# A reordered key scratch read in two loads of 48 rows, and the loads of all x blocks moved behind the tables

## The reference, cut to what matters

```python
q = (x @ wq).reshape(B, S, 16, 16)      # 16 query heads of 16
k = (x @ wk).reshape(B, S, 4, 16)       # 4 key/value heads
v = (x @ wv).reshape(B, S, 4, 16)
q, k = rope(q), rope(k)
scores = einsum('bqkgd,bskd->bkgqs', q.reshape(B, S, 4, 4, 16), k) / 4
out = einsum('bkgqs,bskd->bqkgd', softmax(scores), v).reshape(B, S, 256) @ wo
x = layernorm(x + out)
x = layernorm(x + ffn(x))               # silu gate, 256 -> 1024 -> 256, dequantized integer weights
```

## Time and profile before

| | us |
|---|---|
| median of 3 runs | 902.65 |
| lowest and highest | 902.3, 905.37 |
| profiled execution: its own time | 899.15 |
| profiled execution: span, first to last instruction | 897.3 |
| TensorE busy | 881.7 (98%) |
| VectorE busy | 741.9 (83%) |
| ScalarE busy | 712.9 (79%) |
| GpSimd busy | 268.6 (30%) |
| DMA queue of SP | 50280 packets, 65.53 MB, 28.4% of 16 engines |

### The profile page before, as it was taken

How to read it: one execution, slowest core, us unless ns; L and a number is a source line. 1 busy time by engine, 2 the same in 40 slices (tenths; PEclk the granted TensorE clock), 3 DMA queues, 4 the chain that set the end, 5 groups by cost and what they waited for, 6 DMA issues and landing times.

```text
span 897.3 us, 16216 instructions
## 1 busy us (share of the span) xinstructions
PE 881.7 (98%) x5658; PEld 460.2 (51%) x5658; DVE 741.9 (83%) x1655; ACT 712.9 (79%) x929; POOL 268.6 (30%) x232
## 2 busy tenths in 40 slices
PE   9999999999999999999999999999999999999996
PEld 3334444444444444444444444444436888888885
DVE  5577999999999999999999999999955455665545
ACT  2467999999999999999999999999985566555564
POOL 7763430035434000001001000210104665665555
PEclk9997999999999999999999999999999999999998
DMA  8973553323443132232223313121112010110001
GB/s 265 295 205 113 130 123 79 90 81 77 99 124 61 45 77 64 56 73 67 52 54 85 73 46 78 45 67 32 37 55 57 25 48 24 48 47 25 24 24 48
DMA packets 53458, 69.98 MB, mean 78 GB/s; under 512 B 17344, under 2 KB 26560, under 8 KB 53376
## 3 DMA queue, kind: packets, MB, share of 16 engines
q1 hardware_dynamic: 50280, 65.53, 28.4%
q0 software_dynamic: 864, 3.15, 1.2%
q10 hardware_dynamic: 2232, 0.25, 0.2%
HBM read 46.74 MB, written 16.25 MB: 70 GB/s over the span
## 4 chain that ended last, share of the span: by engine, by line
PE 89%; DVE 4%; ACT 2%; issue 2%; DMA 1%; SPq 1%; POOL 0%; POOLq 0%; DVEq 0%; ACTq 0%
PE pv_bank L1374 26%; PE ring_bank L1286 24%; PE pair_bank L1432 13%; PE pair_bank L1500 12%; PE pv_bank L1526 3%; PE ring_bank L1526 3%; PE ring_bank L1384 2%; PE pair_bank L1320 2%; DVE block_max L851 2%; ACT probs L1187 1%; DMA q_parts<-low 1%; PE ring_bank L1399 1%; PE pv_bank L1338 1%; DVE above L847 0%; PE pv_bank L1264 0%
## 5 line engine op out<-in xcount | busy, mean ns | idle before, releaser
L1187 ACT ACTIVATE probs<-pair_bank 128x1024 f32<-128x1024 f32 x512 | 495.7, 1023 | 43.2 <-PE pair_bank L1432 43.1
L851 DVE TENSOR_REDUCE block_max<-ring_bank 128x1 f32<-128x384 f32 x854 | 486.7, 609 | 15.4 <-PE ring_bank L1286 6.0
L1286 PE MATMUL ring_bank<-k_max,q_sb 48*128 48x512 f32 x1127 | 313.3, 445 | 1.8 <-DVE block_max L847 0.7
L1286 PEld LDWEIGHTS ring_bank<-k_max,q_sb 48*128 48x128 f32 x1127 | 150.2, 185 | 267.5 <-DVE block_max L851 116.8
L1374 PE MATMUL pv_bank<-probs,v_all 128*17 128x512 f32 x2048 | 270.5, 600 | 0.6 <-ACT probs L1187 0.5
L1432 PE MATMUL pair_bank<-q_sb,k_sb 50*128 50x512 f32 x1024 | 221.5, 428 | 1.2 <-ACT probs L1187 0.7
L1042 DVE SCALAR_TENSOR_TENSOR hid<-pair_bank,up_s,silu 128x512 f32<-128x512 f32 x63 | 47.1, 748 | 85.0 <-ACT silu L1243 85.0
L1432 PEld LDWEIGHTS pair_bank<-q_sb,k_sb 50*128 50x128 f32 x1024 | 99.1, 186 | 29.5 <-ACT probs L1187 7.4
L760 POOL TENSOR_TENSOR hid_l<-hid,hid_h 128x512 fp32r<-128x512 f32 x63 | 81.7, 1297 | 86.3 <-ACT hid_h L1222 85.6
L675 POOL TENSOR_TENSOR attn<-attn,inv_rows 128x1024 f32<-128x1024 f32 x7 | 16.7, 2388 | 300.8 <-DMA inv_rows<-inv_d 228.5
L847 DVE CUSTOM_DVE_ANT_0 above<-ring_bank,above 128x512 f32<-128x512 f32 x137 | 94.0, 688 | 5.7 <-PE pair_bank L1286 3.6
(11 more groups left out here) (142 smaller groups left out, 862.0 us busy)
## 6 DMA issues: line engine op xcount, KB each, us to landing
k_max<-k_parts SPq DMA_DIRECT2D x96, 96.0 KB, 3.6
q_sb<-q_parts SPq DMA_DIRECT2D x64, 128.0 KB, 3.4
k_sb<-k_parts SPq DMA_DIRECT2D x96, 64.0 KB, 2.3
attn<-xT SPq DMA_DIRECT2D x8, 512.0 KB, 5.4
q_parts<-high SPq DMA_DIRECT2D x16, 256.0 KB, 3.7
q_parts<-low SPq DMA_DIRECT2D x16, 256.0 KB, 4.1
q_sb<-q_parts SPq DMA_DIRECT2D x64, 64.0 KB, 3.5
attn<-pv_sb SPq DMA_DIRECT2D x128, 32.0 KB
```

The source lines that it names most:

```text
L851: dve.reduce_max(block_max[half % 2][:, col:col + 1], bank[:, 0:width], axis=AX.X).then_inc(ring_used, 1)
L1187: act.activation(probs[t % 2][:, 2 * pr:2 * pr + 2, :], pair_bank[pr][:], ACT.Exp, scale=D ** -0.5).then_inc(probs_ready, 1)
L1286: pe.matmul(bank[:, 0:last - first], q_sb[k][rows, i, qt * P:(qt + 1) * P], k_max[k // QH][rows, kind * CH + first:kind * CH + last], star ...
```

## The change

The scratch of keys gets an axis for the combination, and its order is now sequence, chunk, combination, row, position. The high part is stored twice, as combinations 0 and 1. `load_k` then reads 48 rows in one DMA, once for each row group. A DMA of a key store now covers 64 rows and one chunk, so that `store_k` issues six DMAs instead of two and `store_gap` three instead of two. x blocks 2 to 7 are all issued behind the tables and the identity, and the loads between the stores are gone.

```diff
-K_LOADS = 16 * GROUPS * COMBOS
+K_LOADS = 16 * GROUPS
+K_STORES = 16 * COMBOS * 2
+GAP_STORES = 16 * COMBOS
...
-        k_parts = nc.dram_tensor("k_parts", (B, 2, QH + 1, D * HKV, CH), fp32).ap()
+        k_parts = nc.dram_tensor("k_parts", (B, QH + 1, COMBOS, D * HKV, CH), fp32).ap()
...
             head = UNITS * pair + s
+            src = k_parts[head // HKV, 0:parts].rearrange("c m (d h) t -> c (m d h) t", h=HKV).rearrange("c (n h) t -> h n c t", h=HKV)[head % HKV]
             for r in range(GROUPS):
-                for combo, part in enumerate((0, 0, 1)):
-                    src = k_parts[head // HKV, part, 0:parts].rearrange("c (d h) t -> d h c t", h=HKV)[:, head % HKV]
-                    row = r * GROUP + combo * D
-                    queue.dma_start(dst[s][row:row + D].bitcast(fp32).rearrange("d (c t) -> d c t", c=parts), src).then_inc(done[s], 16)
+                rows = dst[s][r * GROUP:r * GROUP + ROWS].bitcast(fp32).rearrange("n (c t) -> n c t", c=parts)
+                queue.dma_start(rows, src).then_inc(done[s], 16)
...
             load_x(1)
             load_q_tables(1)
-            load_x(2)
             sp.dma_start(ident[:], identity).then_inc(ident_loaded, 16)
+            for m in range(2, BLOCKS):
+                load_x(m)
...
-                for part, buf, ready in ((0, high_k, k_hi_ready), (1, low_k, k_lo_ready)):
+                for buf, ready, combos in ((high_k, k_hi_ready, (0, 1)), (low_k, k_lo_ready, (2,))):
                     sp.wait_ge(ready, b + 1)
-                    sp.dma_start(k_parts[b, part, 0:QH].rearrange("c r t -> (c r) t"), buf[:].bitcast(fp32)).then_inc(k_stored[b], 16)
+                    for combo in combos:
+                        for c in range(QH):
+                            src = buf[c * HKV * D:(c + 1) * HKV * D].bitcast(fp32)
+                            sp.dma_start(k_parts[b, c, combo], src).then_inc(k_stored[b], 16)
...
                 for part, buf, ready in ((0, gap_h, gap_h_ready), (1, gap_l, gap_l_ready)):
                     sp.wait_ge(ready, b + 1)
-                    sp.dma_start(k_parts[b, part, QH], buf[:].bitcast(fp32)).then_inc(gap_stored, 16)
+                    for combo in ((0, 1), (2,))[part]:
+                        sp.dma_start(k_parts[b, QH, combo], buf[:].bitcast(fp32)).then_inc(gap_stored, 16)
...
                         store_gap(0)
-                    if m + 3 < BLOCKS:
-                        load_x(m + 3)
                     if m == 2:
                         first_loads()
```

More of the change, by code:

```diff
@@ L398, in first_loads @@
                 load_q(0, 0, sp)
-                sp.wait_ge(k_stored[0], 16 * 2)
-                sp.wait_ge(gap_stored, 16 * 2)
+                sp.wait_ge(k_stored[0], K_STORES)
+                sp.wait_ge(gap_stored, GAP_STORES)
                 sp.wait_ge(memsets, 6)
@@ L542, in attention @@
                         if k == 0 and p % 2:
-                            sp.wait_ge(k_stored[(p + 1) // 2], 16 * 2)
-                            sp.wait_ge(gap_stored, 16 * 2 * ((p + 1) // 2 + 1))
+                            sp.wait_ge(k_stored[(p + 1) // 2], K_STORES)
+                            sp.wait_ge(gap_stored, GAP_STORES * ((p + 1) // 2 + 1))
                         load_k(k_max, p + 1, k // QH, kmax_loaded, sp)
@@ L628, in high_of_k @@
                 pool.wait_ge(k_rot_ready, b + 1)
-                pool.wait_ge(k_stored[b - 1], 16 * 2)
+                pool.wait_ge(k_stored[b - 1], K_STORES)
                 pool.tensor_copy(high_k[:], rotated_k[:]).then_inc(k_hi_ready, 1)
@@ L638, in gap_of @@
                 pool.tensor_tensor(k_half[:], rotated_k[0:HKV * D, :], k_half[:], ALU.subtract).then_inc(k_gap_ready, 1)
-                pool.wait_ge(gap_stored, 16 * 2 * b)
+                pool.wait_ge(gap_stored, GAP_STORES * b)
                 pool.wait_ge(k_gap_ready, b)
@@ L666, in _ @@
             for b in range(B):
-                pool.wait_ge(k_stored[b], 16 * 2)
-            pool.wait_ge(gap_stored, 16 * 2 * B)
+                pool.wait_ge(k_stored[b], K_STORES)
+            pool.wait_ge(gap_stored, GAP_STORES * B)
             pool.wait_ge(v_used, 2 * B)
```

## The result

| | before | after |
|---|---|---|
| median of 4 runs, us | 902.47 | 929.08 |
| lowest and highest | 902.1, 905.37 | 926.72, 931.12 |
| profiled execution, its own time | 899.15 | 931.12 |

The changed kernel is slower: its time is 1.0287 of that of before, 95% interval 1.0254 to 1.0319, 26.6 us. The forecast was 901.5, with 904.8 as the upper end.

A forecast was written before the change was run, and what follows sets the result against it. TensorE, busy 98% of the span, was taken to bound the kernel, with only the projections open to gain. The 0.80 and 0.35 us gaps sum to 1.15: 902.65 - 1.15 = 901.5 us, range 898.0 to 904.8.

The forecast's parts named there:

- Nothing waits there in a way that a transfer could mend: Attention: TensorE's waits from 80 us on are 1.8 us in total, none on a DMA, so sooner or fewer transfers change nothing.
- The 115.7 us of SP: Attention: given as SP's longest wait, for VectorE's shift, to show that SP stands ahead of its work.
- the cost of nothing for the loads in attention: Attention or beside it: 186 load DMAs become 62, 56 us less of SP's time, costed at nothing.
- TensorE shows waits on a DMA in attention: Sign of being wrong, in attention: it would break the cost of nothing given to SP's part.
- The gain of 1.15 us in the projections: End of projections: TensorE's 0.80 us wait for the first k_max and a 0.35 us gap both go.
- the second gap: TensorE's 0.35 us before 39.68 us, released by ScalarE, late behind a store; it was to go too.
- my bounds (30.5 to 32.5): Start in us of the first k_max loads on SP; the value taken was 31.05.
- The other landing that the prediction names: First k_max: by ports, 48 rows move at most 217 GB/s, landing near 37.4, 0.8 us of the sum unpaid.
- Rival A: Start of attention: the half-clock stretch, some 3 us, goes (898.5 us) or a second comes (904.5); chance 0.2.
- the x blocks in front are paid for: Queue before the first k_max: 1.43 MB added, yet k_max lands at 36.3 us, before TensorE asks at 36.53.
- rival B's late stores: SP's queue, 12 to 38 us: block 0's stores land after 23.6, k_max at 39 to 40; +1.7 to +2.7 us; chance 0.15.
- fifteen more stores in pair 0 fit in: Pair 0 of attention: five more in each of three halves, 3 us each, only shorten SP's waits; cost nothing.

The follow-up runs named there:

- x_back: The changed kernel with the x blocks loaded where they were before; scratch, stores and the two loads of 48 rows stay; 929.5 us, ratio 1.0312.
- x_only: The kernel before with only the loads of the x blocks moved behind the tables; 901.54 us, ratio 0.9982.
- x_late: The kernel before with x blocks moved to the front and k_max in attention loaded only when the next half's shift has landed; 899.44 us, ratio 0.9939.
- x_ahead: The kernel before with x blocks in front and the last shift write moved from ScalarE's queue to SP's, ahead of k_max; 899.61 us, ratio 0.9955.
- late_kmax: The changed kernel with one more SP wait: k_max in attention is loaded only when the next half's shift has landed; 901.66 us, ratio 0.9987.
- shift_ahead: The changed kernel with the last shift write of a half moved from ScalarE's queue to SP's, ahead of k_max; 899.37 us, ratio 0.9956.
- long_rows: The changed kernel with a scratch where a row's chunks are neighbours, so 288 KB come in 48 pieces instead of 144; 922.92 us, ratio 1.0221.
- two_and_one: The changed kernel with each k_max load cut in two DMAs, 192 KB and 96 KB; 910.06 us, ratio 1.0062.
- six_loads: The changed kernel with each key operand loaded from the new scratch by six DMAs of 16 rows instead of two of 48; 907.87 us, ratio 1.0056.

## Why the prediction was wrong, point by point

**"Nothing waits there in a way that a transfer could mend": true of the list of waits, not of the kernel.** The list shows neither what is nearly late nor what is late by a tenth or two. In attention it has no wait on a transfer, and I took that for room. The last shift write had 2.92 us from issue to use at the boundary above, and its landing was what ended them. The 115.7 us of SP that the prediction calls its longest wait are 31 waits, the longest 7.1 us: SP does stand ahead of its work, but that says nothing of a write from ScalarE's queue.

**The step that failed is the cost of nothing for the loads in attention.** "Elsewhere 186 DMAs of such loads become 62 [...] I cost that at nothing." I counted SP's time, which is what merging saves, and looked for who waits behind SP. I did not count what a merged DMA does to the other queue. The text even named the cover whose loss would break it ("TensorE shows waits on a DMA in attention"), and gave it no price and no chance. It should have been a rival: place, each half with `k % QH == 0`; price, the time that 192 KB more take on the DMA engines; point from which it decides, the margin of the last shift write. In hindsight, from part 6 of the two pages: the `k_max` DMAs land after 5.1 us in the median, and after 3.6 before, so some 1.5 us in each of up to 14 halves, some 20 us. Measured were 15.7 us in 12, and 13 us of lower clock behind them. The rows for it were in the trace: both queues' issues around one boundary, and the distance to the matmul that uses them.

**The gain of 1.15 us in the projections didn't come either.** SP did finish its `k_max` issues earlier, at 32.84 instead of 33.73, and the store of q's low part was issued at 33.48 instead of 34.36. The first maximum still came at 37.52 with 0.60 us of wait, for 37.34 with 0.80 in the earlier trace rows (TensorE ended its projections at 36.92 here, for 36.53), and the second gap stayed at 0.33. Of the term of 1.15 us, 0.2 is what the waits became shorter:

```profile
37.52 0.46 PE L1290 MATMUL pair_bank<-k_max,q_sb 48*128 48x512 f32 x1 [0.60 <-DMA k_max<-k_parts]
...
39.84 0.50 PE L1290 MATMUL pair_bank<-k_max,q_sb 48*128 48x512 f32 x1 [0.33 <-ACT above L1134]
```

ScalarE's high part began at 38.67, behind a store that took 5.1 us to land instead of 4.1. What I won in issues was lost in landings. That the large load in front delays the store behind it, as it does the shift later, is the likely reason; no run isolates it here. I had let the landing time stand at what it was while the load grew to three times its size. The two loads were begun at 32.06, inside my bounds (30.5 to 32.5) but a microsecond past the value that I took, because SP's key and gap stores took their issue time there. x_back shows the other half of the account: with the new stores and loads and the x blocks at their old places `k_max` is 2.14 us late and ScalarE waits 4.8 us for its store, while x_only has 0.33 and 2.5. So moving x helped, the stores and the loads took it back. The kernels agree among themselves: x_late and x_ahead, with x_only's projections, wait 0.38 and 0.37 us, and late_kmax and shift_ahead, with the changed kernel's, 0.58 and 0.95. The other landing that the prediction names, near 37.4 with 0.8 us unpaid, fits the start at 37.52, but says nothing of the rows of a load: x_only's six loads of 16 rows give a start at 37.49.

**The clock.** Rival A looked at the half-clock stretch at the start of attention and whether it would go. It is what the waits bring about that mattered: of the 12 waits five were followed by a stretch at the lower clock, 29 us in all, and these cost nearly as much as the waits, 13 us. The stretch at the start neither went nor came from the change. By the Trainium skill (TensorE: Matmul & The Clock Gate, section "HAM oscillation — how this bites in real kernels") idle stretches of TensorE behind a DMA are what sends its clock down, and the penalty is half of the slow time. The trace agrees with the penalty, about 0.45 us for one. For the first it shows that each of the five falls stands behind a wait on a DMA of 1.4 to 1.8 us, and that seven other such waits, of 0.5 to 1.6 us, were followed by none. In long_rows two of 12 were, and of the six in two_and_one none.

**Right** were only that the x blocks in front are paid for (rival B's late stores didn't come: no L1097 waited for a store near 23 to 27 us), and that fifteen more stores in pair 0 fit in, as long as the loads are two; six_loads shows that beside six loads they don't.

## What to carry to other kernels

Merging DMAs saves time on the queue that issues them, and can take it from a small transfer that another queue issues just behind. Before a load is made larger, look for the latest small write on the other queues, measure from its issue to its first use, and put the large load behind it in program order, or cut it. And where the list of waits is empty, read one boundary instruction by instruction: no margin at all looks the same in it as one of ten microseconds.

## What was not expected of the hardware

A small DMA from one queue stands behind a large one that another queue issued just before, and the longer the larger that is. Packets that started in the trace of the changed kernel, by quarter microsecond: `k_max` from SP's queue (2 KB packets) and ScalarE's third and fourth shift writes (16 packets of 128 bytes each, issued at 206.50 and 207.26):

```
from us   k_max   shift from ScalarE's queue
 208.00      0    16
 208.25      0     0
 208.50      3     0
 208.75      5     0
 209.00     25     0
 209.25     35     0
 209.50     38     5
 209.75     23    11
```

The third write moved 1.6 us after its issue. So late after its own the fourth would have moved near 208.9, when 8 packets of `k_max` had been started. It moved after 2.5 us, when 103 had been, most of the 144 of the first DMA. At the other eleven boundaries with a wait 89 to 235 had been, so in six of the twelve some of the second DMA's too, which was issued after the write. In the kernel before the fourth moved 1.7 to 1.8 us after its issue, behind 37 of a DMA's 48 packets. By the Trainium skill (DMA: Bandwidth & Descriptors, section "Issuing engines are not separate DMA queues") DMAs of different engines run on the same 16 DMA engines and interleave: that they share them is what this case shows. By the same page of the Trainium skill (section "Queues, rings and completion order") each DMA engine changes between queues only at the end of a packet, and a packet is typically some 9 to 17 descriptors. A descriptor there is one run of bytes, what this trace lists as a packet. As an estimate from that page: the 144 runs of a `k_max` DMA are 9 for each of 16 engines, so an engine may move its whole share of the DMA before it turns to the small write. The trace agrees with that as far as it goes: the write was never let in among the first runs of the load. It does not tell which engine moved what, so whether this is the reason stays open. That fewer and longer pieces changed little (long_rows) speaks for the bytes.
